# A Mamba-style block on one core: the shared FFN's SiLU beside the other SiLUs, VectorE's side operations between scan and product, GpSimd's products at units 2 and 5

## The reference

```python
# the state space part, 512 channels with 16 states each
xi, z = jnp.split(_layernorm(h) @ W_in, 2, axis=-1)
xc = silu(causal_conv4(xi) + conv_b)
dt, Bm, Cm = jnp.split(xc @ W_x, [16, 32], axis=-1)
delta = jax.nn.softplus(dt @ W_dt + b_dt)
dA = jnp.exp(delta[..., None] * A)
dBu = delta[..., None] * Bm[:, :, None, :] * xc[..., None]
def step(hs, inp):
    dA_t, dBu_t, C_t = inp
    hs = dA_t * hs + dBu_t
    return hs, jnp.einsum('bdn,bn->bd', hs, C_t)
y = scan(step) + xc * D
h = h + (y * silu(z)) @ W_out
# the shared FFN, for every token
x = _layernorm(h)
x1 = x @ sw1.T + sb1
x2 = x @ sw2.T + sb2
sh = _ln(silu(x1) * x2, s_ln_g, s_ln_b)
h = h + sh @ sw3.T + sb3
# 512 chosen tokens also get the best of eight experts, weighted
...
```

## Time and profile before

| | us |
|---|---|
| median of 3 runs | 1729.16 (1728.2 to 1730.28) |
| profiled execution, first to last instruction | 1726.7 |
| GpSimd busy | 1564.6 (91%) |
| VectorE busy | 1555.7 (90%) |
| TensorE busy | 1480.7 (86%) |
| ScalarE busy | 1331.9 (77%) |
| VectorE's 512 scans (L1307) | 656.2 + 392.3 |
| VectorE's 320 products (L1316) | 353.7 |
| GpSimd's 512 dBu (L1646) and 192 products (L1654) | 1075.5 + 409.2 |

### The profile page before, as it was taken

One profiled execution on the slowest core, in us unless ns is written; L12 is line 12 of the kernel. 1 busy time (PEld: TensorE's weight loads), 2 busy tenths in 40 slices (PEclk: granted clock), 3 DMA queues, 4 the chain that ended last, 5 costly groups with the idle time before them and its releaser, 6 DMA issues.

```text
span 1726.7 us, 28038 instructions
## 1 busy us (share of the span) xinstructions
PE 1480.7 (86%) x9868; PEld 1065.4 (62%) x9868; DVE 1555.7 (90%) x1389; ACT 1331.9 (77%) x3100; POOL 1564.6 (91%) x782
## 2 busy tenths in 40 slices
PE   7778898889888988898889889888889898977688
PEld 7555666666666666666666666666666666654355
DVE  2599999999999999999999999999999999999944
ACT  2577788888888888888888888888888888886644
POOL 0699999999999999999999999999999999999814
PEclk9888999999999999999999999999999999997899
DMA  4667755555656655656666555566665555656110
GB/s 141 138 135 180 163 130 123 122 131 132 145 129 146 132 123 122 131 130 146 129 146 135 122 125 126 130 146 129 145 138 121 125 126 129 142 119 141 36 34 15
DMA packets 194430, 218.47 MB, mean 127 GB/s; under 512 B 94011, under 2 KB 184773, under 8 KB 193778
## 3 DMA queue, kind: packets, MB, share of 16 engines
...
...
q10 hardware_dynamic: 192, 0.01, 0.0%
...
## 4 chain that ended last, share of the span: by engine, by line
DVE 41%; ACT 18%; issue 16%; PE 13%; POOL 10%; DMA 2%; SPq 0%; DVEq 0%; ACTq 0%; POOLq 0%
DVE psum L1307 20%; DVE xr L1307 16%; ACT psum L1010 6%; POOL xr L1646 6%; POOL xr L1654 3%; PE psum L610 3%; DVE xr L1316 3%; ACT L1132 2%; PE psum L697 2%; PE psum L782 2%; ACT L1041 2%; ACT soft L1062 2%; ACT soft L1066 2%; ACT soft L1058 2%; PE psum L783 1%
## 5 line engine op out<-in xcount | busy, mean ns | idle before, releaser
L1646 POOL TENSOR_TENSOR xr<-u,bbc 128x912 f32<-128x912 f32 x512 | 1075.5, 2133 | 14.3 <-DMA u<-u_scratch 13.9
L1010 ACT ACTIVATE psum<-delta,a_neg 128x228 f32<-128x228 f32 x2048 | 805.9, 441 | 221.6 <-DVE xr L1316 191.2
L1307 DVE TENSOR_TENSOR_SCAN psum<-psum,xr 128x912 f32<-128x912 f32 x320 | 656.2, 2051 | 68.5 <-ACT psum L1010 59.8
L1654 POOL TENSOR_TENSOR xr<-xr,cbc 128x912 f32<-128x912 f32 x192 | 409.2, 2131 | 31.9 <-DVE xr L1307 28.5
L1307 DVE TENSOR_TENSOR_SCAN xr<-psum,xr 128x912 f32<-128x912 f32 x192 | 392.3, 2043 | 0.0
L1316 DVE TENSOR_TENSOR xr<-psum,cbc 128x912 f32<-128x912 f32 x320 | 353.7, 1105 | 11.1
L711 PE MATMUL psum<-xr,fold 128*32 128x228 f32 x4096 | 295.1, 385 | 50.6 <-POOL xr L1654 26.7
L610 PE MATMUL psum<-xh,win 128*128 128x228 f32 x1024 | 222.7, 367 | 61.8 <-ACT xs L1041 33.4
L610 PEld LDWEIGHTS psum<-xh,win 128*128 128x128 f32 x1024 | 192.1, 193 | 91.7 <-ACT xs L1041 44.0
L661 PE MATMUL psum<-xi,conv_d 128*128 128x228 f32 x1024 | 210.9, 358 | 0.0
L711 PEld LDWEIGHTS psum<-xr,fold 128*32 128x32 f32 x4096 | 96.9, 112 | 178.1 <-issue 79.4
...
## 6 DMA issues: line engine op xcount, KB each, us to landing
delta<-delta_scratch SPq DMA_DIRECT2D x256, 228.0 KB, 6.5
u<-u_scratch SPq DMA_DIRECT2D x256, 228.0 KB, 4.2
bbc<-bc_scratch SPq DMA_DIRECT2D x128, 114.0 KB, 2.6
...
cbc<-bc_scratch SPq DMA_DIRECT2D x128, 114.0 KB, 2.7
...
```

What stands on the lines that cost most here:

```text
L1010: ins = nc.scalar.activation(slot(k)[:, j * TOK:(j + 1) * TOK], delta4[:, c // 2, j, c % 2], ACT.Exp, scale=a_neg[:, c, j, n:n + 1])
L1307: nc.vector.tensor_tensor_scan(x if k in ON_POOL else slot(k), slot(k), x, 0.0, ALU.mult, ALU.add).then_inc(scan_done, 1)
L1646: nc.gpsimd.tensor_tensor(xr[:, k % XRING], u4[:, c // 2, :, c % 2], bbc[:, p, n].unsqueeze(1).to_broadcast([P, J, TOK]), ALU.mult).then_i ...
L1654: nc.gpsimd.tensor_tensor(xr[:, k % XRING], xr[:, k % XRING], cbc[:, p, k % NI].unsqueeze(1).to_broadcast([P, J, TOK]), ALU.mult).then_inc ...
```

## The change

It has four parts.

1. `ON_POOL` is now a table with one row, (2, 5, 8, 10, 12, 14): GpSimd makes the products of units 2 and 5, VectorE those of units 1 and 3. `on_pool(g)`, `pool_products(g, k)` and `dve_products(g, k)` count the products so far; the waits in `product_done`, `exps` and elsewhere use them.
2. In groups 0 to 28 (`in_window`) the sigmoid from three activations goes. ScalarE copies x1 and x2 from PSUM to a new tile `f12` at unit 14 (`ffn_copy`), and in the next loop's window, between the SiLUs of x and z, makes SiLU of x1 + b1 in place (`ffn_silu`). VectorE then makes v in one operation, `ffn_product`, from the two halves of `f12`, at unit 1 of loop g + 3. The projection of z waits for the copy and no longer for v. Groups 29 to 31 keep the old form.
3. On VectorE side operations now stand behind the scan of their unit and ahead of its product: the second layer norm's moments at unit 0, y's second half and `ffn_product` at unit 1, the image tokens at unit 3, y's first half at unit 11 (it was at 10).
4. For group 29 `ffn_gate` is cut in two, one half ahead of product 15 and one behind it.

```diff
-ON_POOL = (1, 3, 8, 10, 12, 14)
+ON_POOL = ((2, 5, 8, 10, 12, 14),)
...
-            gate = sb("gate", [P, TOK])
-            vv = sb("vv", [P, TOK])
+            f12 = sb("f12", [P, 2, TOK])
...
                         elif runs(g - 3):
-                            pe.wait_ge(v_done, g - 2)
+                            pe.wait_ge(f12_ev, g - 2)
...
-                        if back in ON_POOL:
+                        if step < 0 or back in on_pool(step):
                             need(act, scan_done, v - SLOTS + 1)
                         else:
-                            need(act, c_dve, N_DVE * step + ON_DVE.index(back) + 1)
+                            act.wait_ge(c_dve, dve_products(step, back) + 1)
...
+                    def ffn_copy(g):
+                        act.wait_ge(f12_mm, g + 1)
+                        need(act, f3_mm, g)
+                        nc.scalar.activation(f12[:], f12_ps(g), ACT.Copy).then_inc(f12_ev, 1)
+
+                    def ffn_silu(g):
+                        act.wait_ge(f12_ev, g + 1)
+                        nc.scalar.activation(f12[:, 0], f12[:, 0], ACT.Silu, bias=b1[:, 0:1]).then_inc(fs_done, 1)
...
+                        if runs(i - 3) and in_window(i - 3):
+                            ffn_silu(i - 3)
                         if runs(i):
                             z_silu(i, p, 0)
                             z_silu(i, p, 1)
...
                             if k == 14 and runs(i - 2):
-                                ffn_sigmoid(i - 2)
+                                (ffn_copy if in_window(i - 2) else ffn_sigmoid)(i - 2)
...
+                    def ffn_product(g):
+                        dve.wait_ge(fs_done, g + 1)
+                        nc.vector.scalar_tensor_tensor(out=f12[:, 1], in0=f12[:, 1], scalar=b2[:, 0:1], in1=f12[:, 0],
                                                        op0=ALU.add, op1=ALU.mult).then_inc(v_done, 1)
...
                         for k in range(UNITS):
-                            if k == 1 and runs(i - 2):
-                                ln2_ready(i - 2)
                             if runs(i):
                                 scan(i, k)
+                            if k == 0 and runs(i - 2):
+                                ln2_ready(i - 2)
+                            if k == 0 and runs(i - 2):
+                                ln2_moments(i - 2)
+                            if k == 1 and runs(i - 1):
+                                y_out(i - 1, q, 1)
+                            if k == 1 and runs(i - 3) and in_window(i - 3):
+                                ffn_product(i - 3)
                             if k == 3 and runs(i + 2):
                                 image_tokens(i + 2)
-                            if k == 1 and runs(i - 1):
-                                y_out(i - 1, q, 1)
+                            if k == 7 and runs(i + 1):
+                                delta_out(i + 1)
                             if k == 9 and runs(i + 2):
                                 normalize(i + 2, p)
-                            if k == 7 and runs(i + 1):
-                                delta_out(i + 1)
+                            if k == 11 and runs(i):
+                                y_out(i, p, 0)
+                            if k == 15 and runs(i - 2) and not in_window(i - 2):
+                                ffn_first(i - 2)
                             if runs(i):
                                 times_c(i, p, k)
```

More of the change, by code:

```diff
@@ L49, in fusion_kernel, with on_pool, pool_products, dve_products @@
     E = gate_w.shape[2] - 1
-    ON_DVE = tuple(k for k in range(UNITS) if k not in ON_POOL)
-    N_DVE, N_POOL = len(ON_DVE), len(ON_POOL)
+    def on_pool(g):
+        return ON_POOL[g % len(ON_POOL)]
+    def pool_products(g, k):
+        return sum(len(on_pool(a)) for a in range(g)) + sum(x < k for x in on_pool(g))
+    def dve_products(g, k):
+        return UNITS * g + k - pool_products(g, k)
+    ALL_DVE = dve_products(GROUPS, 0)
     bc_scratch = nc.dram_tensor("bc_scratch", (2, 2 * NS, TOK), F32, kind="Internal").ap()
@@ L226, in gate_of @@
             def gate_of(g):
-                return {GROUPS - 2: sq[:, 0], GROUPS - 1: xh[:, 0, 0]}.get(g, gate[:])
+                return {GROUPS - 2: sq[:, 0], GROUPS - 1: xh[:, 0, 0]}.get(g, f12[:, 0])
             def vv_of(g):
-                return {GROUPS - 2: sq[:, 1], GROUPS - 1: xh[:, 0, 1]}.get(g, vv[:])
+                return {GROUPS - 2: sq[:, 1], GROUPS - 1: xh[:, 0, 1]}.get(g, f12[:, 1])
             def ffn_free(e, g):
@@ L238, in ffn_free, with in_window @@
                     e.wait_ge(z_mm, 2 * GROUPS)
+            def in_window(g):
+                return g < GROUPS - 3
             def ffn_bank(g):
@@ L379, in fusion_kernel @@
             h2n_done = sem("h2n_done")
+            f12_ev = sem("f12_ev")
             fe_done = sem("fe_done")
@@ L436, in product_done @@
             def product_done(e, i, k):
-                if k in ON_POOL:
-                    e.wait_ge(c_pool, N_POOL * i + ON_POOL.index(k) + 1)
+                if k in on_pool(i):
+                    e.wait_ge(c_pool, pool_products(i, k) + 1)
                 else:
-                    e.wait_ge(c_dve, N_DVE * i + ON_DVE.index(k) + 1)
+                    e.wait_ge(c_dve, dve_products(i, k) + 1)
             with nc.Block() as block:
@@ L1306, in scan @@
                         x = xr[:, k % XRING].rearrange("p j t -> p (j t)")
-                        nc.vector.tensor_tensor_scan(x if k in ON_POOL else slot(k), slot(k), x, 0.0,
+                        nc.vector.tensor_tensor_scan(x if k in on_pool(i) else slot(k), slot(k), x, 0.0,
                                                      ALU.mult, ALU.add).then_inc(scan_done, 1)
                     def times_c(i, p, k):
-                        if k in ON_POOL:
+                        if k in on_pool(i):
                             return
-                        if k == ON_DVE[0]:
+                        if dve_products(i, k) == dve_products(i, 0):
                             dve.wait_ge(c_in, 16 * NQ * (i + 1))
@@ L1375, in ffn_gate, with ffn_first @@
                     def ffn_gate(g):
+                        ffn_first(g)
+                        ffn_second(g)
+                    def ffn_first(g):
                         dve.wait_ge(fs_done, g + 1)
@@ L1379, in ffn_gate, with ffn_second @@
                                                        op0=ALU.add, op1=ALU.mult).then_inc(gate_done, 1)
-                        dve.wait_ge(gate_done, g + 1)
+                    def ffn_second(g):
+                        dve.wait_ge(gate_done, g - (GROUPS - 4))
                         if g < GROUPS - 2:
@@ L1684, in body @@
                         for k in range(UNITS):
-                            if runs(i) and k in ON_POOL:
+                            if runs(i) and k in on_pool(i):
                                 times_c(i, p, k)
```

21 lines of the change are left out of this document (9 added, 12 removed).

## The result

The changed kernel takes 1872.35 us (median of 4 runs, 1871.3 to 1878.16) against 1728.84 us for the kernel before (median of 4): a ratio of 1.0835, 95% interval 1.0819 to 1.0851. It is slower by 143.5 us; the forecast was 1727.5, in a range of 1699 to 1738. The profiled execution spans 1871.0 us against 1726.7, a difference of 144.3.

A forecast was written before the change was run, and what follows sets the result against it. Bound: VectorE's 40.17 us, then ScalarE's 9.09, 49.26 a group. Held ffn_product makes a ring of 49.4; -3.2 - 0.75 + 3.65 + 0.6 - 1.9 = -1.6 us off the median 1729.16 gives 1727.5, range 1699 to 1738.

The forecast's parts named there:

- The place and the due time: On VectorE, ffn_product follows y at unit 1, due at T+7.1, after GpSimd's dBu of unit 4 starts at T+6.61.
- T: The end of product 15 on VectorE in a group; ScalarE's turn follows, forecast at 9.09 us to the next S.
- stands until its end at T+8.74: ffn_product, with two SBUF inputs, is held by GpSimd only until the running dBu ends; forecast chance 0.60.
- second rival: GpSimd's next dBu takes the ports first, so ffn_product waits one operation more; ring 51.5, about 1785 us; chance 0.12.
- its one row: At the program's end, VectorE's 0.17 us operation took 0.64, to 1705.79, while GpSimd's L1727 ran to 1705.76.
- The rest of the sum: Ring from S to S: 10.67 + 35.36 + 3.31 = 49.34, or 49.55; taken as 49.4, +0.14 us a group.
- the ends: First and last groups: groups 0 to 2 -3.2 us, group 3 -0.75, group 30 +0.6, group 31 and tail -1.9.
- S: The start of scan 2 on VectorE in a group; S to S is the time of one group, 49.26 us before.
- A sign that it named: The prediction called itself wrong at its root if, among other signs, S to T isn't near 39.4.
- S to T: VectorE's stretch from scan 2's start to product 15's end: 40.17 us before, forecast 39.42.
- first rival: ffn_product is not held by GpSimd, or slips into the gap; 48.51 us a group, 1703.5 us; chance 0.22.
- the softplus stall: VectorE reaches the delta operation at S+15.59, softplus is ready at S+16.23: a new wait of about 0.7 us.

The follow-up runs named there:

- e13: Changed kernel, but GpSimd waits for its own last dBu (unit 4) ahead of the dBu of unit 5; 1729.17 us, ratio 1.0004.
- e7: Kernel before with only the FFN part of the change, GpSimd keeping products 1 and 3 and side operations their old places; 1950.25 us in the profiled run.
- e4: Changed kernel, but GpSimd waits for v (ffn_product) ahead of the dBu of unit 5; 1728.56 us, ratio 0.9998.
- e5: Changed kernel, but GpSimd waits for v (ffn_product) ahead of the dBu of unit 4; 1706.02 us, ratio 0.9870.
- e3: Changed kernel, but TensorE makes the tokens of group i+2 ahead of v_center(i-3); 1786.89 us, ratio 1.0337.
- e1: Changed kernel, but ffn_product's second input is scan 1's result in PSUM instead of the SiLU in SBUF; 1705.83 us, ratio 0.9865.

## Why the prediction was wrong

- **The place and the due time were right.** y waits 0.74 for TensorE, ffn_product is issued at T+7.10 (forecast T+7.1), into the dBu of unit 4 (869.01, T+6.4; forecast T+6.61), and it needs 0.25 behind GpSimd (forecast 0.24).
- **The step that failed** is "stands until its end at T+8.74". VectorE was passed over there and let in one operation later, at T+10.56, when GpSimd stood idle. This is the second rival's mechanism; the prediction named the boundary as the point that decides, saw that its one row had nothing queued behind it, and still gave the forecast 0.60 and the rival 0.12. The row couldn't tell the two apart, and the odds should have been nearer to even. In the kernel before, GpSimd's next operation there began at 1705.87, 0.11 behind 1705.76, so the boundary even had a gap, as in e13. The Trainium skill (SBUF — State Buffer, "Summary: rules for kernel authors") says of a VectorE instruction with two SBUF inputs and a GpSimd instruction that reads SBUF that the second one to issue is blocked until the first finishes. Read as a wait that ends with that one instruction, this falls short here as the forecast does: the wait ran over up to four GpSimd instructions (7.32 us in e7), and the measurement decides.
- **The rest of the sum** holds in the main. With the gap that the forecast took for granted, e4 and e13 have 49.37 in most groups (forecast 49.4) and take 1728.56 and 1729.17 us. That the totals lie so near to 1727.5 is in part luck: in e4 the two long groups cost about 5.7 us, and the ends differ from the forecast. S of group 3 comes 1.35 earlier than before (forecast 3.2), and what follows S of group 30 is 2.25 shorter (forecast 1.3).
- **A sign that it named** came true: S to T isn't near 39.4 but 42.84 (819.80 to 862.64). Of the 3.42 more, 3.18 lie ahead of product 5 (S+13.85 where S+10.67 was forecast), behind the late v. Without the hold (e5) S to T is 39.48, as forecast.
- **The second rival's price** was 51.5 and about 1785 us (its own terms, with the ends of the sum, give 1782). e3 measured 51.42 and 1786.89, with TensorE's v_center out of the way. The price left out who waits for v in order: the tokens behind v_center, the lower clock behind that wait, and through B and C v_norm: 3.18 us a group, 27 x 3.18 = 86 us.
- **The first rival** (48.5, 1703.5 us) is what an operation that isn't held gives: 48.61 in e1 and e5, 1705.83 and 1706.02. In e5, S to T is 39.48 (scan 2 at 750.15, product 15 ended at 788.52 + 1.11 = 789.63; forecast 39.42) and T to S 9.09 (forecast 9.09), the softplus stall 0.73 (forecast 0.7). In the changed kernel that stall is 0.39, since VectorE is late there by itself.
- **GpSimd's step** stays 2.08 and its work 47.84 a group. The loss is in the ring of waits, not in work. One figure of the prediction is off by a hundredth: its terms give T+8.73 for the end of the dBu, not T+8.74.
